# Matrix build of a graph network: the one-hots of the edge messages made on ScalarE, and one place fewer in VectorE's one-hots

## What is computed

```python
# layer 0, for every edge e = (src, dst):
msg_in = concat([x[src], edge_attr])            # 128 + 64
h = relu(msg_in @ W1.T + b1)                    # 128
messages = h @ W2.T + b2
agg = segment_sum(messages, dst)                # then a GRU step on x
# layers 1 to 3 (five convolutions), all over the same edges:
out = segment_sum(x[src] * norm, dst) @ W + b   # norm from degrees, in layer 3 from edge weights too
```

## Time and profile before

| | us |
|---|---|
| median of 3 runs | 5015.88 |
| lowest and highest | 5004.13, 5068.07 |
| span of the profiled execution, first to last instruction | 4951.5 |
| TensorE, VectorE, ScalarE, GpSimd busy | 3982.0, 2602.2, 1548.4, 2555.5 |
| indirect gathers of the matrix build (L951), 832 | 953.8 |
| edge one-hots on VectorE (L707), 208 | 87.6 |

### The profile page before, as it was taken

The page is one execution under the profiler, slowest core; times in us unless marked ns, Lnnn a source line. Parts: engine busy times, 40 slices in busy tenths (PEclk is TensorE's granted clock), DMA queues, the critical chain, the costliest instruction groups (busy, mean ns, idle before and its releaser), DMA issues. The chain is left out here.

```text
span 4951.5 us, 80811 instructions
## 1 busy us (share of the span) xinstructions
PE 3982.0 (80%) x30230; PEld 2665.0 (54%) x30230; DVE 2602.2 (53%) x5064; ACT 1548.4 (31%) x3170; POOL 2555.5 (52%) x2363
## 2 busy tenths in 40 slices
PE   5787787787788887388887886899888899887888
PEld 5677776677677775244443343444444455443444
DVE  7676555555555556555452334355435556513554
ACT  3334554445455564100000000223134334302332
POOL 4665544554555520266645664566256556505663
PEclk6777878888788888699998998899999999988999
DMA  4445555555566664699976664778655555527776
GB/s 147 125 130 163 190 188 182 189 188 189 186 193 200 196 211 147 188 321 322 303 255 188 204 206 140 272 277 291 223 179 186 175 179 176 190 93 259 261 276 244
DMA packets 612892, 1019.37 MB, mean 206 GB/s; under 512 B 90888, under 2 KB 417575, under 8 KB 612111
## 3 DMA queue, kind: packets, MB, share of 16 engines
q1 hardware_dynamic: 476700, 773.91, 45.6%
q0 software_dynamic: 90848, 199.74, 13.9%
q10 hardware_dynamic: 44956, 40.55, 2.6%
HBM read 737.12 MB, written 276.78 MB: 205 GB/s over the span
## 5 line engine op out<-in xcount | busy, mean ns | idle before, releaser
L951 POOL DMA_INDIRECT x<-p_table,src_i x832 | 953.8, 1146 | 826.0 <-DVE x L711 541.3
L1540 POOL DMA_INDIRECT rows_b<-x_table,low_src x552 | 585.0, 1060 | 540.5 <-POOLq L159 203.6
L930 ACT CAST st_cnt<-ps_mat 128x512 bf16<-128x512 f32 (+1 forms) x825 | 445.7, 585 | 520.8 <-PE ps_deg L845 239.7
L1619 PE MATMUL po_l3b<-mat_l3b,rows_b 128*128 128x512 f32 (+1 forms) x1372 | 580.7, 570 | 32.5 <-DMA mat_l3b<-weights_fwd 25.2
L1540 POOL DMA_INDIRECT rows_a<-h_table,low_src x412 | 441.7, 1072 | 302.1 <-DVE split_l3b L1831 178.2
L860 PE MATMUL ps_mat<-rows_a,hot_s 128*128 128x128 bf16 x4851 | 416.6, 244 | 135.1 <-issue 97.7
L860 PEld LDWEIGHTS ps_mat<-rows_a,hot_s 128*128 128x128 bf16 x4851 | 337.6, 111 | 180.1 <-issue 118.3
L1619 PE MATMUL po_l3a<-mat_l3a,rows_a 128*128 128x512 f32 (+1 forms) x882 | 390.5, 589 | 47.0 <-DMA mat_l3a<-weights_fwd 37.2
L1619 PE MATMUL po_l3c<-mat_l3c,rows_a 128*128 128x512 f32 (+1 forms) x882 | 390.5, 590 | 29.3 <-DMA mat_l3c<-weights_fwd 25.2
L1619 PEld LDWEIGHTS po_l3b<-mat_l3b,rows_b 128*128 128x128 f32 x1372 | 247.6, 200 | 258.5 <-issue 231.4
L1619 PE MATMUL po_l<-mat_l,rows_a 128*128 128x512 bf16 (+1 forms) x1323 | 298.2, 380 | 106.3 <-DVE mat_l L1859 87.1
(11 more groups left out here) (419 smaller groups left out, 7215.9 us busy)
## 6 DMA issues: line engine op xcount, KB each, us to landing
weights_fwd<-st_wt SPq DMA_DIRECT2D x396, 256.0 KB
mat_l<-counts_fwd SPq DMA_DIRECT2D x112, 896.0 KB
mat_l3a<-weights_fwd SPq DMA_DIRECT2D x56, 1792.0 KB
mat_l3c<-weights_fwd SPq DMA_DIRECT2D x56, 1792.0 KB
counts_rev<-st_cnt SPq DMA_DIRECT2D x588, 128.0 KB
rev_l<-counts_rev SPq DMA_DIRECT2D x84, 896.0 KB
mat_l3b<-weights_fwd SPq DMA_DIRECT2D x42, 1792.0 KB
counts_fwd<-st_cnt SPq DMA_DIRECT2D x396, 128.0 KB
```

Of the source, the lines that this page charges most:

```text
L930: nc.scalar.copy(st_cnt[:, q, :, j * 2 * P:j * 2 * P + n_col], ps_mat[:, f % 3, :].rearrange("p (d c) -> p d c", d=2)[:, :, 0:n_col]).then ...
L951: pool.indirect_dma_start(ring[:, j % RING, t * FD:(t + 1) * FD], None, p_table, bass.IndirectOffsetOnAxis(src_i[:, j * TH + t:j * TH + t ...
L1540: pool.indirect_dma_start(ring[:, j % RL, t, :], None, table, bass.IndirectOffsetOnAxis(low_src[:, j * TH + t:j * TH + t + 1].bitcast(U32), 0)
L1619: mm = nc.tensor.matmul(po[:, p % 2, k, 0:nb * P].rearrange("p (d c) -> p d c", c=P), rows[:, s, k * P:(k + 1) * P], cols, start=(s == 0 a ...
```

## The change

ScalarE makes the edge one-hots, in edge_hots(j), called right behind the message ReLU of the same half step. A square with a bias column gives (local - i) squared over the 64 window positions i, once per tile, that is four instructions into a new tile off; one ReLU over all four tiles then gives relu(1 - off), which is 1 where local = i and 0 elsewhere. ScalarE waits for step_sum as VectorE did, for its own last one-hot and for the last square. VectorE's L707 goes; its wait for step_sum stays in message_sum. In one_hots the second half has 11 places in place of 12: place 25, the self loops, gets no one-hots.

```diff
--- before.py
+++ after.py
@@ -540,6 +540,7 @@
             msg = x_room[:, RING * TH * FD:(RING + 4) * TH * FD].rearrange("p (q e) -> p q e", q=4)
             edge = rows_a[0:ED + 1, 8 * P * HALF:8 * P * HALF + 4 * TH * P].rearrange("p (h e) -> p h e", h=2)
             hot = sb("hot", [P, 4, TH, W], F32, c)
+            off = sb("off", [P, TH, W], F32, c)
             st_cnt = sb("st_cnt", [P, STAGES, 2, 4 * P], BF16, c)
             st_wt = sb("st_wt", [P, STAGES, 4 * P], F32, c)
             deg_in = sb("deg_in", [P, NB, 4], F32, c)
@@ -561,7 +562,7 @@
             gathered = [sem(f"gathered{q}") for q in range(RING)]
             edge_in = [sem(f"edge_in{h}") for h in range(2)]
             edge_mul, pre_done, msg_done, passed = sem("edge_mul"), sem("pre_done"), sem("msg_done"), sem("passed")
-            hot_ready, step_sum, added = sem("hot_ready"), sem("step_sum"), sem("added")
+            hot_ready, step_sum, added, off_ready = sem("hot_ready"), sem("step_sum"), sem("added"), sem("off_ready")
             staged_out = [sem(f"staged_out{q}") for q in range(STAGES)]
             rec_copied, rec_moved, nodes_in, xt_ahead = sem("rec_copied"), sem("rec_moved"), sem("nodes_in"), sem("xt_ahead")
             count_ready, counted = sem("count_ready"), sem("counted")
@@ -679,7 +680,7 @@
 
                     def one_hots(u, h):
                         m = 2 * u + h
-                        n = 2 * HALF if h == 0 else NK + 1 - 2 * HALF
+                        n = 2 * HALF if h == 0 else NK - 2 * HALF
                         ks = slice(2 * HALF * h, 2 * HALF * h + n)
                         if h == 0:
                             dve.wait_ge(slots_ready, 2 * u + 1)
@@ -704,8 +705,6 @@
                         if j >= 4:
 
                             dve.wait_ge(step_sum, j // 2 - 1)
-                        V.tensor_tensor(hot[:, j % 4], per_block(iota_row[:, 0:W], TH),
-                                        per_row(local0[:, j * TH:(j + 1) * TH], W), ALU.is_equal).then_inc(hot_ready, 1)
                         dve.wait_ge(gathered[j % RING], 16 * TH * (j // RING + 1))
                         dve.wait_ge(edge_mul, j + 1)
                         V.tensor_tensor(msg[:, j % 4], pm[:, j % 2], ring[:, j % RING], ALU.add).then_inc(pre_done, 1)
@@ -916,6 +915,18 @@
 
                 @block.scalar
                 def _(act):
+                    def edge_hots(j):
+                        if j >= 4:
+                            act.wait_ge(step_sum, j // 2 - 1)
+                        if j:
+                            act.wait_ge(hot_ready, j)
+                        for t in range(TH):
+                            mark = nc.scalar.activation(off[:, t, :], iota_row[:, 0:W], ACT.Square, scale=-1.0,
+                                                        bias=local0[:, j * TH + t:j * TH + t + 1])
+                        mark.then_inc(off_ready, 1)
+                        act.wait_ge(off_ready, j + 1)
+                        nc.scalar.activation(hot[:, j % 4], off[:], ACT.Relu, scale=-1.0, bias=ones[:, 0:1]).then_inc(hot_ready, 1)
+
                     for n in range(UN):
                         (u, s), q = divmod(n, SUBS), n % STAGES
                         w = sub_cols(s)
@@ -938,6 +949,7 @@
                             if e is not None and e < HS:
                                 act.wait_ge(pre_done, e + 1)
                                 nc.scalar.activation(msg[:, e % 4], msg[:, e % 4], ACT.Relu).then_inc(msg_done, 1)
+                                edge_hots(e)
                     act.wait_ge(filled, fills_before(NB) + 1)
                     nc.scalar.copy(rec[:, :, 7], weight[:]).then_inc(rec_copied, 1)
                     act.wait_ge(rec_copied, 1)
```

## The result

The changed kernel took 5120.03 us (median of 4 runs, 5103.09 to 5131.08), the one before on the same chip 5014.94 (4 runs, 5004.13 to 5068.07): ratio 1.017, 95% interval 1.013 to 1.022. Forecast were 5096 us, within a range from 4985 to 5200, and the sign was right. The 64 us that the prediction laid around the span were a misreading: the profiled execution after lasted 5122.06 us with a span of 5120.0, so 2 us lie around a span, and the profiled execution before, with its span of 4951.5, was simply 1.2% quicker than its median, and quicker than all four runs. A comparison of the two profiles therefore overstates the change (168 us between the spans, 105 between the medians). Where the 168 us lie is seen in three windows of each profile: the narrow blocks, the wide ones, and everything behind the build.

What follows compares the result with a forecast made beforehand. The prediction took the build's engine ring, closed in wide blocks by ScalarE's PSUM evictions, as the bound. Wide +82, narrow +9 and -11 us, clock 0, gave +80: span 5031 plus 64 around it, 5096 us, range 4985 to 5200.

Steps and rivals of the forecast that it cites:

- The 64 us that the prediction laid around the span: Whole kernel: median 5015.88 us less profiled span 4951.5, taken as time around the span and added to the forecast span.
- The ring and who waits in it: Matrix build: three engines wait in a ring, closed in wide blocks by ScalarE's PSUM evictions; TensorE idles 236 us there.
- The price of 1.5 us an event: ScalarE behind each message ReLU: four squares and one ReLU add 1.5 us, 208 times, 312 us of ScalarE time.
- The narrow blocks: 11 us of gain from VectorE, 9 us of loss: Narrow blocks, 44 events: half of VectorE's 22 us saving gained, ScalarE's work costing 0.2 us an event.
- 0.5 us of 1.5 exposed in each wide event, 82 us: Wide blocks, 164 events: 0.5 us of ScalarE's added work reaches TensorE each time; bounds 0 and 246 us.
- the step that expected some 80 us more of it before L840 and L860: Wide blocks: TensorE's idle time before these two matmuls rises some 80 us between 500 and the stage's end.
- all hidden: Rival: fills behind the ReLU lose nothing, about 5000 us; decided by idle before L840 and L860 staying near 236; chance 0.27.
- The clock, taken as 0 with a far end of 40 us: Wide blocks: longer waits may lower TensorE's granted clock, 13 us per 0.01; taken as 0, far end 0.03.
- a sign of being wrong: Wide blocks: granted clock below 0.79, listed beside a block period of 45 us or of 50 us and more.
- The walk along the ReLUs: Eleven ReLUs between 1100 and 1195 us, slack before eviction and fill read: 6.0 us exposed, 0.55 each, taken as 0.5.
- All of it exposed (0.20): Rival: TensorE waits the full 1.5 us at each wide event, price 224 us, time 5240; chance 0.20.
- ScalarE: Activation LUTs, rules for kernel authors: Edge one-hots: rule puts relu, add and multiply on VectorE; by it alone the move costs 225 us, time 5240.

Runs made afterwards that it cites:

- act_extra: Kernel before, with ScalarE also making the edge one-hots behind the message ReLU into a tile nobody reads; VectorE's kept: 4415.0 us, ratio 1.043.
- no_hots: Kernel before with edge one-hots made on neither engine (tile zeroed once) and the self-loop place dropped: 4229.48 us, ratio 0.9985.
- place_only: Kernel before with only the self-loop place's one-hots dropped, edge one-hots staying on VectorE: 4231.64 us, ratio 1.001.
- act_only: Changed kernel with the self-loop place kept, so only the edge one-hots move to ScalarE: 4442.13 us, ratio 1.050 to the kernel before.
- after_again: The changed kernel unaltered, run again on a faster chip: 4436.96 us, ratio 1.047 to the kernel before.
- relu_at_edges: Kernel before, self-loop place dropped, with only ScalarE's message ReLU moved behind the evictions of event e + 2's place: 4226.79 us, ratio 0.998.
- at_edges: Changed kernel with ScalarE's message ReLU and one-hots moved behind the evictions of event e + 2's place: 4281.05 us, ratio 1.0115 to the kernel before.

## Why the prediction was right, point by point

- **The ring and who waits in it.** Right. TensorE waits for evictions, VectorE for TensorE; act_extra shows the cost with nothing but ScalarE's work added, no_hots that VectorE's work is worth next to nothing. One reading was too round: of the 209 us of VectorE's idle time before L688 the row names TensorE for 172, and 36 are "remote".
- **The price of 1.5 us an event.** Right: squares of 0.342 us (0.34 forecast), the ReLU 0.508 (0.51).
- **The narrow blocks: 11 us of gain from VectorE, 9 us of loss.** Neither shows on the faster chips: the median of no_hots is 2 us below before (15 at most) and that of place_only the same, and place_only and act_only have the same narrow blocks, 2584 and 2580 products between 90 and 370 us. On the first chip this part failed: forecast were 2 us less, and the narrow blocks took 38 us more, or 34 by the estimate above, at a clock of 0.64 instead of 0.71. That is a third of the whole loss. A single pair of profiles doesn't tell how much of it is the change, and its cause stays open.
- **0.5 us of 1.5 exposed in each wide event, 82 us.** On the first chip the number comes near (93 us in the profiles, some 75 by the estimate above), but not by its mechanism, so that it fits there is luck. The term was read as idle time, and the step that expected some 80 us more of it before L840 and L860 failed: it grew by 0.7 us a block, 23 us, and TensorE's idle time as a whole by 3 us over all wide blocks. The rest is busy time. By the prediction's own test (idle time before these two that stays near 236 us; it is 170.8 + 69.6 = 240 now) the rival "all hidden" would have won, and the kernel was slower even so. On the faster chips the mechanism holds: 102 us more idle time over 164 events is 0.6 us an event.
- **The clock, taken as 0 with a far end of 40 us.** This is the term that was mis-sized. On the first chip the granted clock of the wide stretch fell by 0.05, and by my own price of 13 us for each 0.01 that is 65 us; it went to 0.77, below the 0.79 that the prediction had named as a sign of being wrong. On the faster chips it fell by 0.09 and the products took 3.6 us a block longer, 119 us of 207 (108 over the whole stage). The Trainium skill, TensorE: Matmul & The Clock Gate ("Why this matters for your kernels"), has the rule that idle gaps cost clock. On the faster chips the direction agrees, though the page's row is about gaps longer than any in the wide blocks of after_again, where TensorE's longest is 1.7 us. On the first chip idle time doesn't explain the fall, since it was 292 us before and 295 after; what pulled the clock down there stays open. The prediction should have carried a share of the clock in the sum.
- **The walk along the ReLUs.** On the faster chips it is a fair tool for idle time. Done over all 166 ReLUs of the wide blocks in place_only, it gives 57, 87 and 119 us for 0.9, 1.2 and 1.5 us of added work; TensorE's idle time grew by 40, 68 and 95. What it can't see is the busy time, 89 us of the full dose. For the old ReLU it would have promised some 20 us (40 of 166 are followed at once by an eviction and a waiting fill, 0.5 us each); relu_at_edges shows 4 us by the medians, with an interval up to 19.
- **All of it exposed (0.20).** Its number is near that of the faster chips, 207 us against 224, but its mechanism isn't: it asked for the full 1.5 us of waiting at each event, and TensorE's idle time grew by 0.6. The other half is slower products.
- **ScalarE: Activation LUTs, rules for kernel authors.** The Trainium skill's rule, that such simple operations belong on VectorE, is borne out here. The reason isn't only the price of a set of one-hots (0.421 us against 1.6), since at_edges pays the same price for a quarter of the loss; it is which engine the others wait for.

What stays open: why the change costs 1.017 on one chip and 1.047 on others. A wide block took 44.6 us before on the first chip and 31.9 on a faster one, so the first may leave ScalarE more slack between events, which would hide more of the 1.5 us. The walk speaks against it: over all wide ReLUs it gives 112 us on the first chip and 119 on the other. None of the ten experiments ran on the first chip, so the explanation by waits and clock is shown for the faster chips alone.

## What to carry to other kernels

Before work is moved off an engine, see who waits for it: here VectorE was waiting for TensorE, and 105 us less work on it were worth nothing that could be measured, while 1.5 us on the engine that empties PSUM cost about 1 us each time (0.5 on the first chip). If such work must go there, put it where the product engine has other things to do than fill PSUM: the same instructions cost 51 us in one place of the queue and 207 in another. And count the clock beside the waits: with the full dose of short waits TensorE's products themselves became slower, and that was half of the loss.

## What the runs showed of the hardware that was not expected

- The same kernel took 5015 us on one chip and 4231 on another, with granted clocks of 0.869 in the profile on the first and 0.930 on the other (place_only). A profile is worth most beside runs of its own chip.
- The granted clock of the wide blocks didn't fall evenly with the added work: 0.97, 0.98, 0.96 and 0.90 for 0, 0.9, 1.2 and 1.5 us an event, with 62, 102, 130 and 157 us of TensorE's idle time in them. The mean weight-sum product, between 450 and 1350 us, went with it from 222 to 235 ns. Only the last step is clear: kernels that take the same time (place_only, relu_at_edges, no_hots) show 0.97, 0.96 and 0.99 in single profiles. At which point the clock falls, no run here settles.
- Spans and device times lie 2 us apart, but one profiled execution may stand 1.2% from the median of its kernel.
